# First attention's row maxima as products of 64 rows in two halves of TensorE's array

## What is computed

```
q = ln @ Wq.T                                     # 2 x 1024 x 256, 4 heads of 64
kv = concat([xn @ Wkv.T, ln @ Wlkv.T], axis=1)    # 77 context rows and 1024 latent rows
qn = rmsnorm(q, qn_g) * SCALE
kn = rmsnorm(k, kn_g)
attn = einsum('bhid,bhjd->bhij', qn, kn)          # 1024 queries x 1101 keys, depth 64
attn = where(mask, attn, -max); attn = softmax(attn)
out  = einsum('bhij,bhjd->bhid', attn, v); out = out @ Wo.T + bo
```

## Time and profile before

| | us |
|---|---|
| median of 3 runs | 823.34 (822.98 to 825.36) |
| the profiled execution | 826.39 |
| its span, first to last instruction | 824.5 |
| PE busy, PEld, DVE, ACT, POOL in the span | 760.7, 621.4, 528.5, 399.1, 319.7 |

### The profile page before, as it was taken

One profiled execution on the slowest core, in us unless ns is written; L12 is line 12 of the kernel. 1 busy time (PEld: TensorE's weight loads), 2 busy tenths in 40 slices (PEclk: granted clock), 3 DMA queues, 4 the chain that ended last, 5 costly groups with the idle time before them and its releaser, 6 DMA issues.

```text
span 824.5 us, 12845 instructions
## 1 busy us (share of the span) xinstructions
PE 760.7 (92%) x4881; PEld 621.4 (75%) x4881; DVE 528.5 (64%) x1163; ACT 399.1 (48%) x699; POOL 319.7 (39%) x281
## 2 busy tenths in 40 slices
PE   8889989999999999999999899983799999999996
PEld 7755546656755554679889888882788999999996
DVE  7767875773677683357455498975746656667552
ACT  3655634573465344563462244433034765557551
POOL 5502001200301022066361053334235878787783
PEclk9999999999999999999999999995699999999998
DMA  7000000000000100100030201121212444544532
GB/s 186 1 0 1 1 0 1 1 0 1 1 1 2 51 4 0 52 1 3 1 98 1 103 2 52 52 77 39 103 34 78 132 119 147 129 116 110 142 33 32
DMA packets 21509, 39.31 MB, mean 48 GB/s; under 512 B 4913, under 2 KB 16905, under 8 KB 19145
## 3 DMA queue, kind: packets, MB, share of 16 engines
q1 hardware_dynamic: 14793, 30.07, 11.1%
q0 software_dynamic: 6656, 8.43, 5.9%
HBM read 29.96 MB, written 8.40 MB: 47 GB/s over the span
## 4 chain that ended last, share of the span: by engine, by line
PE 56%; DVE 15%; ACT 4%; issue 3%; POOL 3%; another core or an unknown queue 0%; DVEq 0%; ACTq 0%
PE ps L481 18%; PE ps L650 8%; PE ps L1173 5%; PE ps L1176 5%; PE ps L754 5%; PE ps L671 2%; PE ps L672 2%; PE ps L612 2%; PE ps L475 1%; DVE sm L1613 1%; DVE rep L1807 1%; PE ps L1096 1%; DVE Pb L1617 1%; DVE sm L1622 1%; POOL out_dram L2724 1%
## 5 line engine op out<-in xcount | busy, mean ns | idle before, releaser
L650 PE MATMUL ps<-PT,VA 128*65 128x512 f32 (+1 forms) x288 | 147.5, 594 | 2.8 <-ACT PT L2116 2.5
L2116 ACT ACTIVATE PT<-ps 128x512 f32<-128x512 f32 x128 | 76.0, 594 | 62.0 <-PE ps L672 61.7
L481 PE MATMUL ps<-GT,wh 128*128 128x258 f32 (+1 forms) x768 | 94.6, 284 | 0.4 <-DVE GT L1905 0.4
L481 PEld LDWEIGHTS ps<-GT,wh 128*128 128x128 f32 x768 | 92.7, 189 | 0.6 <-DVE GT L1905 0.6
L2724 POOL DMA_INDIRECT out_dram<-ye,idx x40 | 67.2, 1679 | 19.9 <-issue 10.9
L2410 ACT ACTIVATE het<-ps,b1e 128x514 f32<-128x514 f32 x64 | 44.1, 689 | 61.4 <-PE ps L481 53.7
L1940 DVE TENSOR_TENSOR he<-het,he 128x514 fp32r<-128x514 f32 x64 | 45.6, 713 | 40.2 <-ACT he L1969 38.2
L671 PE MATMUL ps<-QA,KA 128*128 128x512 f32 x144 | 67.5, 468 | 0.8 <-ACT QB L1969 0.8
L2460 POOL TENSOR_TENSOR rs<-rs,half 128x4 f32<-128x4 f32 (+2 forms) x19 | 18.2, 956 | 123.5 <-DVE rs L1214 95.6
L612 PE MATMUL ps<-KA,QA 128*128 128x368 f32 x192 | 59.2, 414 | 4.4 <-DVE x L1422 2.1
L2602 POOL DMA_INDIRECT gt<-y_dram,idx x40 | 46.3, 1158 | 43.3 <-DVE gate L1895 33.5
(11 more groups left out here) (291 smaller groups left out, 1654.2 us busy)
## 6 DMA issues: line engine op xcount, KB each, us to landing
wr<-in_w1e_dram SPq DMA_DIRECT2D x8, 1024.0 KB, 5.0
wr<-in_w2e_dram SPq DMA_DIRECT2D x8, 1024.0 KB
x<-in_x_dram SPq DMA_DIRECT2D x4, 512.0 KB, 6.2
w<-in_w_dram SPq DMA_DIRECT2D x2, 1024.0 KB, 4.7
y_dram<-yr SPq DMA_DIRECT2D x3, 512.0 KB, 3.0
out_dram<-x SPq DMA_DIRECT2D x3, 512.0 KB, 4.1
b2r<-in_b2r_dram SPq DMA_DIRECT2D x8, 128.0 KB, 3.3
gt<-y_dram,idx POOLq DMA_INDIRECT x40
```

What stands on the lines that cost most here:

```text
L481: op = pe.matmul(o, l, r, start=n == 0, stop=n == len(calls) - 1)
L650: pe.matmul(bank[6 + hf][0:65, :], VA[b][0:K, kt, h, :], PT[u % 4][0:K, :], start=kt == 0, stop=kt == 8).then_inc(p_pv, 1)
L2116: a.activation(PT[u % 4][0:K, :], bank[4 + u % 2][0:K, :], ACT.Exp, bias=0.0 if K == 128 else mcol[:, b:b + 1]).then_inc(a_exp, 1)
```

## The change

`max_tile` no longer uses the low keys: it multiplies high queries by high keys alone, over 64 rows. The second copy of the high keys (KB) is moved to partitions 64 to 127, so that it meets the second copy of the high queries there. Columns 1024 to 1103 (the context) and 512 to 1023 are multiplied in partitions 64 to 127, columns 0 to 511 in partitions 0 to 63. There are still three products for a tile, of 80, 512 and 512 columns. The first four tiles of head 0 stay as they were. QB's low queries move to partitions 64 to 127, its maxima to row 0, its rows 1 to 63 are zeroed once by GpSimd, and KB's rows 0 to 63 are all set to one; the second product of the scores now runs over 128 rows. VectorE reduces 80 and 1024 columns where it reduced 368 and 736. `again_k` of the second keys moves ahead of the two high queries on ScalarE, `low_q` of the second queries moves one step later on VectorE. TensorE waits for all three banks ahead of the first product, and for KB's semaphores at a head's first tile.

```diff
-        QB = RA("QB", [65, H0, S], F32R)
+        QB = RA("QB", [128, H0, S], F32R)
-        KB = RA("KB", [65, H0, NK], F32R)
+        KB = RA("KB", [128, H0, NK], F32R)
@@ tensor_program, max_tile
                 if qt == 0:
                     pe.wait_ge(v_ka, 2 * hi + 2)
+                if qt == (0 if hi else 4):
+                    pe.wait_ge(a_kb, 2 * hi + 2)
+                    pe.wait_ge(a_kc, hi + 1)
                 if qt == 4:
                     pe.wait_ge(v_qb, 2 * hi + 2)
-                for j in (2, 0, 1):
-                    clear(j)
-                    op = pe.matmul(ps[:, j, 0:368], QA[:, h, 128 * qt:128 * qt + 128], KA[:, h, 368 * j:368 * j + 368],
-                                   start=True, stop=True)
+                qc = slice(128 * qt, 128 * qt + 128)
+                if hi == 0 and qt < 4:
+                    for j in (2, 0, 1):
+                        clear(j)
+                        op = pe.matmul(ps[:, j, 0:368], QA[:, h, qc], KA[:, h, 368 * j:368 * j + 368], start=True, stop=True)
+                        if j == 2:
+                            op.then_inc(p_m3, 1)
+                    op.then_inc(p_mx, 1)
+                else:
+                    for j in (2, 0, 1):
+                        clear(j)
+                    pe.matmul(bank[2][:, 0:80], QA[64:128, h, qc], KB[64:128, h, 1024:1104], start=True, stop=True).then_inc(p_m3, 1)
+                    pe.matmul(bank[0], QA[0:64, h, qc], KA[0:64, h, 0:512], start=True, stop=True)
+                    pe.matmul(bank[1], QA[64:128, h, qc], KB[64:128, h, 512:1024], start=True, stop=True).then_inc(p_mx, 1)
+                for j in range(3):
                     busy[j] = (v_mx if j < 2 else v_m3, 8 * hi + qt + 1)
-                    if j == 2:
-                        op.then_inc(p_m3, 1)
-                op.then_inc(p_mx, 1)
@@ vector_program, low_q, head, max_tile
-                v.tensor_tensor(QB[0:64, h, c], bank[at_bank["head", H, gi]][64:128, :], f(QA[64:128, h, c]),
+                v.tensor_tensor(QB[64:128, h, c], bank[at_bank["head", H, gi]][64:128, :], f(QA[64:128, h, c]),
                 low_k(H, 1).then_inc(v_ka, 1)
                 yield
+                yield
                 low_q(H, 1)
-                yield
                 yield
-                v.tensor_reduce(mxp[:, qt, 1:2], ps[:, 2:3, 0:368], AX.XY, ALU.max).then_inc(v_m3, 1)
+                whole, context = (368, 368) if hi == 0 and qt < 4 else (512, 80)
+                v.tensor_reduce(mxp[:, qt, 1:2], ps[:, 2:3, 0:context], AX.XY, ALU.max).then_inc(v_m3, 1)
-                v.tensor_reduce(mxp[:, qt, 0:1], ps[:, 0:2, 0:368], AX.XY, ALU.max).then_inc(v_mx, 1)
+                v.tensor_reduce(mxp[:, qt, 0:1], ps[:, 0:2, 0:whole], AX.XY, ALU.max).then_inc(v_mx, 1)
@@ scalar_program, again_k, high_ctx, head, and the first maxima
-                copy(KB[0:64, h, c], f(KA[0:64, h, c])).then_inc(a_kb, 1)
+                copy(KB[64:128, h, c], f(KA[0:64, h, c])).then_inc(a_kb, 1)
-                copy(KB[0:64, h, 1024:1104], kc[0:64, 0:80], gg[0:64, 2:3]).then_inc(a_kc, 1)
+                copy(KB[64:128, h, 1024:1104], kc[0:64, 0:80], gg[0:64, 2:3]).then_inc(a_kc, 1)
                 high_k(H, 1)
+                again_k(H, 1)
+                yield
                 high_q(H, 1, 0)
                 yield
                 high_q(H, 1, 1)
-                yield
-                again_k(H, 1)
                 yield
             a.wait_ge(p_mT, 1)
-            copy(QB[64:65, 0, 0:512], bank[0][64:65, :], -1.0).then_inc(a_mrt, 1)
+            a.wait_ge(g_init, 7)
+            copy(QB[0:1, 0, 0:512], bank[0][64:65, :], -1.0).then_inc(a_mrt, 1)
@@ gpsimd_program
-            g_.memset(f(KB[64:65, :, :]), 1.0).then_inc(g_init, 1)
+            g_.memset(f(KB[0:64, :, :]), 1.0).then_inc(g_init, 1)
             root_c(0)
+            g_.wait_ge(g_init, 6)
+            g_.memset(f(QB[0:64, :, :]), 0.0).then_inc(g_init, 1)
             low(wo[1], wo_in, wo[0], 3)
@@ sync_program, max_row
-                sp.dma_start(f(QB[64:65, h, c].rearrange("p (a q) -> p a q", a=4)), f(mrt[i][hf][:, :])).then_inc(d_mrow[2 * i + hf], 16)
+                sp.dma_start(f(QB[0:1, h, c].rearrange("p (a q) -> p a q", a=4)), f(mrt[i][hf][:, :])).then_inc(d_mrow[2 * i + hf], 16)
```

## The result

The changed kernel takes 833.5 us (median of 4 runs, 831.32 to 835.11) against 823.16 us; the ratio is 1.0118, with a 95% interval of 1.0089 to 1.0147: 10.3 us slower. The profiled execution took 835.11 us, 1.6 us over that median, with a span of 833.1.

What follows compares the result with a forecast made beforehand. PE was taken as the bound most of the time, VectorE in stretches. 46 tiles at +0.34 us gave +15.6 us, other terms 0: profiled 826.4 to 842.0 us, less 3.1 for the median, 838.9 us; range 831 to 848 us.

Steps and rivals of the forecast that it cites:

- the height: PE going from 128 rows to 64 or back: 0.09 us emptying plus 0.11 us exposed load, 0.20 us each change.
- The rival that fp32r would go free of it: Height change costs nothing in fp32r: tile 0.45 or 0.34 us, kernel 821.0 or 816.0 us; chance 9%.
- The step that took it from fp32 to fp32r: No fp32r product of 64 rows in the trace; cost bounded by 0 and 0.20 us, 0.20 taken from fp32 rows.
- The tile: PE's maxima tile in `max_tile`: 0.50 us becomes 0.84 us, +0.34, halves overlapping but loads in turn.
- the second rival: Halves together and their loads too: +0.23 us a tile, 10.6 us, kernel 833.9 us; chance 22%.
- How many tiles count: 60 of 64 tiles change; at 76% in the chain, 46 count, 15.6 us; upper end 20.4 us.
- The columns: Split 3 x 368 to 80 + 512 + 512, the same 1104: something falls away only if both 512 products run together.
- The edits at nothing: 128-row second score product, GpSimd's memsets, new waits, three-bank wait and order in `head`: each taken as 0.
- the order in `head`: `again_k` ahead of `high_q`, second `low_q` a step later: taken as 0, bounds 0 and 4.2 us.
- the memset: GpSimd's new memset of QB, 3.5 us from 25.5 to 29.1 us, in idle time: nothing.
- VectorE's part: Second reduction ends 0.2 us later; in 14 tiles where VectorE carries the chain 0 to 2.8 us, taken as 0.

Runs made afterwards that it cites:

- e1: Kernel before with its three products of 368 columns cut to 64 rows, one half, nothing else changed: 842.25 us, ratio 1.021.
- e5: Changed kernel with the old three products of 368 columns over 128 rows and old reductions, all other edits kept: 823.88 us, ratio 1.0015 to the kernel before.
- e9: Changed kernel with keys split 368, 368, 368 over upper, lower, upper half and VectorE's reductions as before: 833.36 us, ratio 1.0123 to the kernel before.
- e8: Changed kernel with the old order in `head` (`again_k` last on ScalarE, `low_q` a step earlier): 835.69 us, ratio 1.0149 to the kernel before.
- e10: Changed kernel with TensorE's pause before the attention filled by extra transposes: 834.57 us, ratio 1.0142 to the kernel before.
- e7: Changed kernel with the two 512-column products first, the 80 columns last, VectorE reducing 1024 first: 836.95 us, ratio 1.0178 to the kernel before.
- e4: Changed kernel with all three products in the lower half, partitions 0 to 63: 854.01 us, ratio 1.0349 to the kernel before.
- e6: Kernel before with columns split 80, 512, 512 over 128 rows, reduced as 80 and 1024, no other edits: 830.63 us, ratio 1.0086.
- e3: Changed kernel with its 80, 512 and 512 columns multiplied over all 128 rows, other edits kept: 835.53 us, ratio 1.012 to the kernel before.
- e2: Kernel before with its three products of 368 columns cut to 65 rows: 828.7 us, ratio 1.0041.
- e12: e3 with TensorE's pauses filled by transposes, around the first maxima and before two layer norm turns: 830.1 us, ratio 1.0074 to the kernel before.
- e11: Kernel before with TensorE's pause before the attention filled by the same transposes as e10: 824.07 us, ratio 1.0006.

## Why the prediction was right

**Direction and mechanism** were right, for the height. PE stands on each way between 128 and 64 rows, and with equal columns that alone makes the kernel slower (e1, e5 against e9). The rows of fp32 products gave the price to the hundredth: 0.09 + 0.11 us each way, seen in e1 as twice 0.20 on fp32r. The rival that fp32r would go free of it is out. The step that took it from fp32 to fp32r had no row behind it, but held.

**The tile was sized too large.** I let the loads of the two halves follow each other and got 0.84 us. They start at the same moment (192.41 twice), so the tile is 0.73 us: +0.23, not +0.34. That is the second rival, halves together and loads too, and its 833.9 us is 0.4 us from the measured 833.5; so close a hit is in part luck, since its near equals e8 and e10 came out at ratios of 1.0149 and 1.0142, 2.0 to 2.6 us more than the changed kernel's 1.0118. The page behind it, the Trainium skill's "TensorE: Matmul & The Clock Gate", Part 3, has loads and products in different row groups overlap, and a load with a running product only where the row groups differ. On the first the trace agrees: the two first loads start together. On the second the measurement decides: with 128 rows, too, the next load starts as the product before it does. Its 4 ns between the starts of such products is not what this pair shows: the second product of 512 columns starts 0.13 us after the first in the trace (192.41, 192.54), since its half had been given to the 80 columns and needs a load again. In e7, where the pair comes first and both halves have just been loaded, its two products start 0.003 us apart (188.995 and 188.998), which agrees with that figure. e4 showed the two halves together directly, by 0.24 us a tile.

**How many tiles count.** I took 76%, 46 of 60, from the chain. The profile without a fall of the clock (e10) has +9.6 us for 60 x 0.23 = 13.8: 70%, 42 tiles. In the stretch without falls it is 71% for the changed kernel, 72% for e9, 76% for e1 and 84% for e4: near the 76%, and somewhat more for a longer tile. That the rest lies in pauses of PE was supposed, not tested. With my own tile of 0.84 the share of 70% gives 14 us, so most of the 5.4 us between forecast and result is the loads.

**The columns** were a term put at nothing without a reason that held: 1104 columns in either case, so only the overlap would count. But 80 columns do not cover a load, and over 128 rows the split costs 7.1 us by itself (e6), of which its tiles explain 4.2 at most. In the sum this did no harm: the tile in 64 rows had its loads counted one by one, and beside that tile the split costs little more (e9 against e10). What it changes is the reading of the loss. Of the 9.6 us in e10's stage 7.0 are there without any change of height, and the height adds 2.6; with equal columns it adds 8.4 to 8.7 by the same stages, its fall taken off (e5, e9).

**The edits at nothing** cost about 1 us together (e5), the order in `head` nothing (e8), the memset lay in a pause of GpSimd, from 25.5 to 29.0 us. VectorE's part, taken as 0 with 2.8 as its bound, is 0 within some 0.2 us in the profiles (e9, e10).

**What I left out** is the clock. PE is at its lower level for 3.4 or 6.8 us now and then behind a pause, and each 3.4 us cost 1.4 to 1.7 us. In the changed kernel it changes no verdict; in e3 it made up 3 to 4 of 10 us, and from the medians alone one would conclude that the height costs nothing.

No version tried beats the kernel before. A tile that makes the detour alone cannot get under it, by an estimate from these figures: two ways at 0.20 us and 552 columns in either half (0.24 us) make 0.64 us against 0.50. Two tiles in one detour would come to 0.88 us against 1.00 by the same estimate; no run tried that.

## What to carry to other kernels

Packing two products of 64 rows saves half the streaming, but going into that height and back costs 0.40 us here; it pays only where more than that is saved in one go, which for fp32r is over 900 columns of overlap (0.40 us at 0.44 ns a column), so the thing to try is to group many such products together. Products of 65 rows instead of 64 show no switch in the trace (e2). A product that is shorter than a weight load (0.11 us, about 250 columns) between others leaves the next load in the open, so over 128 rows equal pieces are better than two full banks and a rest (e5 against e6); in the two halves it made no difference (e9). Before reordering such a product look at which bank then comes free last. And two changes made together need not add up: test each with the other held equal.

## What was not expected of the hardware

- Loads into the two halves start together (192.41 us twice), while two loads into the same half lie 0.11 us apart (e4). So with 64 rows two loads fit into the time of one.
- The granted clock fell to its lower level for 3.4 us, or 6.8, behind pauses of PE of 1.4 to 2.0 us in otherwise full work (in e12 at 86 us behind three of 0.3 to 0.9 us), in some profiles and not in others with the same pause: in e3 at 40, 112 and 126 us, in e11 at 107.5 us behind a pause of 1.81 us, which the kernel before has at the same place, 1.80 us long, without a fall. In e12 there was no fall at the places that transposes filled whose results nobody reads, and its median is 3.8 us lower than e3's; in e10 and e11 such a fill was worth nothing.
- 80 columns of fp32r stream in 0.04 us (e3, e7), the same rate per column as 512.
